# Row norms that travel as rows through DRAM instead of a second turn of the attention output

## The reference

```python
def xattn(q, k, v, Wq, Wk, Wv, Wo, bo, g):            # q = layernorm(x), k = v = ctx
    qh, kh, vh = (einsum('bcn,oc->bon', t, W) in 8 heads of 64)
    qh = softmax(qh, axis=-2) * SCALE
    kh = softmax(kh, axis=-1)
    context = jnp.einsum('bhdn,bhen->bhde', kh, vh)
    out = jnp.einsum('bhde,bhdn->bhen', context, qh)
    out = jnp.einsum('bcn,oc->bon', out, Wo) + bo[None, :, None]
    norm = jnp.maximum(jnp.sqrt(jnp.sum(out * out, axis=1, keepdims=True)), 1e-12)
    return out / norm * g * np.sqrt(DIM)

def ffn(x, c1_w, c2_w, w1, w2t):                      # x: 2048 rows of 512
    inter = xf @ c1_w.T @ c2_w.T                      # 1792 columns
    idx = argmax of each block of 32 columns
    h = relu(w1[idx] . xf)                            # 56 values per row
    return h @ w2t[idx]

x = x + xattn(layernorm(x), ctx, ctx, ...)
x = x + ffn(layernorm(x), ...)
```

## Time and profile before

| | before |
|---|---|
| median of 3 runs | 752.01 us (751.99 to 753.22) |
| profiled execution | 753.24 us, span 751.3 us |
| TensorE busy | 98% |
| VectorE busy | 83% |
| GpSimd busy | 65% |
| ScalarE busy | 53% |
| mean granted TensorE clock | 0.995 |

### The profile page before, as it was taken

How to read it: one execution, slowest core, us unless ns; L and a number is a source line. 1 busy time by engine, 2 the same in 40 slices (tenths; PEclk the granted TensorE clock), 3 DMA queues, 4 the chain that set the end, 5 groups by cost and what they waited for, 6 DMA issues and landing times.

```text
span 751.3 us, 14646 instructions
## 1 busy us (share of the span) xinstructions
PE 737.9 (98%) x5210; PEld 563.4 (75%) x5210; DVE 623.5 (83%) x910; ACT 401.7 (53%) x773; POOL 485.9 (65%) x549
## 2 busy tenths in 40 slices
PE   8999999999999999999998999999999999999998
PEld 6566565565665665666667999999898999989896
DVE  6999999999999999999968677887777878777652
ACT  4899999999999999998840111111111210211110
POOL 3789999999998888687666254543545355263420
PEclk9999999999999999999998999999999999999999
DMA  7223434334333323222211203031130312111011
GB/s 167 72 79 106 121 97 119 108 101 127 98 96 102 97 78 104 75 72 57 65 40 29 73 20 106 21 101 25 26 104 20 106 21 72 56 24 50 20 52 34
DMA packets 66376, 55.23 MB, mean 74 GB/s; under 512 B 40704, under 2 KB 49536, under 8 KB 66304
## 3 DMA queue, kind: packets, MB, share of 16 engines
q1 hardware_dynamic: 65568, 53.44, 26.0%
q10 hardware_dynamic: 736, 0.85, 0.5%
HBM read 38.52 MB, written 8.39 MB: 62 GB/s over the span
## 4 chain that ended last, share of the span: by engine, by line
PE 68%; POOL 23%; DVE 2%; SPq 2%; issue 2%; ACT 1%; DMA 1%; POOLq 0%; DVEq 0%
PE slot L1109 20%; PE po L1127 11%; PE turn L1127 11%; POOL Q L535 9%; PE po L1237 6%; PE turn L1222 4%; POOL weights_lo L484 4%; PE turn L1205 4%; PE slot L1263 3%; PE slot L1277 3%; POOL c_low L517 3%; POOL x_low L474 3%; POOL weights_hi L482 2%; SPq L276 2%; PE slot L1091 2%
## 5 line engine op out<-in xcount | busy, mean ns | idle before, releaser
L423 POOL TENSOR_TENSOR E<-E,rank 128x512 bf16<-128x512 bf16 (+1 forms) x64 | 71.0, 1110 | 110.8 <-DVE E L621 109.8
L535 POOL TENSOR_TENSOR Q<-Q,qrec 128x1024 f32<-128x1024 f32 x64 | 121.1, 1903 | 31.6 <-DVE qrec L773 31.6
L1237 PE MATMUL po<-E,ctxT 128*64 128x512 f32 x256 | 116.9, 599 | 0.0
L1240 PE MATMUL po<-QT,G 128*64 128x512 f32 x256 | 116.9, 599 | 0.0
L939 ACT ACTIVATE E<-slot,neg_kmax 128x512 f32<-128x512 f32 x128 | 86.3, 686 | 10.8 <-DVE neg_kmax L759 10.7
L725 DVE TENSOR_REDUCE qmax<-slot 128x16 f32<-128x1024 f32 x64 | 75.3, 1217 | 12.3 <-PE slot L1277 12.3
L1237 PEld LDWEIGHTS po<-E,ctxT 128*64 128x64 f32 x256 | 32.3, 136 | 64.9 <-issue 58.7
L436 POOL TENSOR_TENSOR behind<-E,first 128x512 bf16<-128x512 bf16 (+1 forms) x64 | 60.1, 941 | 31.8 <-DVE first L629 31.7
L765 DVE TENSOR_REDUCE qsum<-Q 128x16 f32<-128x1024 f32 x64 | 77.3, 1208 | 3.1 <-ACT Q L928 1.9
L759 DVE TENSOR_REDUCE neg_kmax<-slot 128x2 f32<-128x1024 f32 x64 | 76.3, 1192 | 1.0
L947 ACT ACTIVATE E<-turn 128x512 f32<-128x512 f32 x128 | 74.9, 612 | 3.1 <-PE turn L1205 2.1
(11 more groups left out here) (185 smaller groups left out, 1961.2 us busy)
## 6 DMA issues: line engine op xcount, KB each, us to landing
c_in<-in_ctx SPq DMA_DIRECT2D x64, 128.0 KB, 2.7
x_in<-in_x SPq DMA_DIRECT2D x64, 128.0 KB, 2.6
stage<-in_ffn_w SPq DMA_DIRECT2D x32, 225.0 KB, 2.6
out<-E SPq DMA_DIRECT2D x16, 256.0 KB, 2.3
ctxT<-in_ctxT SPq DMA_DIRECT2D x31, 128.0 KB, 2.4
attn_out<-po_sb SPq DMA_DIRECT2D x31, 128.0 KB, 2.3
attn<-attn_out SPq DMA_DIRECT2D x9, 256.0 KB, 3.7
E<-attn_out SPq DMA_DIRECT2D x7, 256.0 KB, 4.4
```

The costliest lines, as they stand in the source:

```text
L535: nc.gpsimd.tensor_tensor(half, half, qrec[1 - par][:, s, :].unsqueeze(2).broadcast_to([P, HALF, D]), ALU.mult).then_inc(q_scaled, 1)
L1237: nc.tensor.matmul(po[0:C, :], ctxT[1 - par][:, m, :], E[1 - par][:, :, m * P:(m + 1) * P], start=(m == 0), stop=(m == NT - 1)).then_inc(p ...
L1240: nc.tensor.matmul(po[C:P, :], G[:, m, :], QT[m][:], start=(m == 0), stop=(m == HT - 1)).then_inc(out_mm, 1)
```

## The change

The attention output is no longer scaled in its turned form and no longer turned back. It is still turned once to get the sums of squares, but ScalarE squares it in place in PSUM and VectorE reads the sums from there, ordered by batch. GpSimd's power then works on one tile (tiles 0, 1) or on two tiles at once (128x16). TensorE turns the 8 or 16 columns of factors with a single transpose (`turn_factors`), ScalarE copies them to SBUF as rows of 128 (`keep_rows`), a DMA stores them to a new DRAM tensor `factors`, and after it has landed, DMAs load them back, each row of 512 repeated over the 64 channels of its batch. VectorE (GpSimd for tiles 0 and 1) multiplies the unturned attention output by that. In the duos the two DMA trips are issued from ScalarE's queue (`exchange`), in the attention steps from SyncE's.

Orders change too. Tiles 0 and 1 begin in steps 24 and 27 (before 27 and 29), their factors travel in steps 25 and 28, and their normalization is GpSimd's. In the duos `turn_attn` of tiles a + 2 and a + 3 comes one duo earlier, after `down(d, 3)`, with squares and norms behind it; `turn_factors` stands before `hide(d, 1)`. GpSimd's `select(2)`, `rank_mask(3)` and `rank_mask(4)` move to the end of the duo before, and VectorE's order follows. SyncE's load of the next attention tiles waits for the residual, before the masks 6 and 7.

```diff
+TURNS = (B - 8, B - 5)
+        over_channels = lambda a, b: factors[a, b:b + 1].broadcast_to([C, N])
+        inverted = lambda a: a + 1 if a < 2 else 2 + a // 2
```

On SyncE:

```diff
+                def store_factor(a):
+                    sp.wait_ge(rows_kept, a + 1)
+                    sp.dma_start(rows_of(factors[a]), inv_rows[0:2 * NT, :]).then_inc(first_stored, 16)
+                def load_factor(a):
+                    sp.wait_ge(first_stored, 16 * (a + 1))
+                    for b in range(2):
+                        sp.dma_start(spread_of(a)[b * C:(b + 1) * C, :], over_channels(a, b)).then_inc(spread_in[a], 16)
...
-                    if known == B - 2:
-                        sp.wait_ge(norm_sum, 2)
+                    if known == TURNS[1] + 2:
+                        sp.wait_ge(scaled, 2)
                         load_xr(1)
...
                         sp.dma_start(scratch[g - 2], po_sb[par][C:P, :]).then_inc(stored[par], 16)
+                    if known == TURNS[0] + 1:
+                        sp.wait_ge(c2_done, C2_ITEMS)
+                        store_factor(0)
+                        load_factor(0)
+                    if known == TURNS[0] + 2:
+                        sp.wait_ge(rank_done, 1)
+                        load_attn(1)
+                    if known == TURNS[1] + 1:
+                        sp.wait_ge(added, 1)
+                        store_factor(1)
+                        load_factor(1)
...
                         for a in (2 * d + 4, 2 * d + 5):
-                            sp.wait_ge(attn_turned, a - 1)
+                            sp.wait_ge(added, a - 1)
                             load_attn(a)
```

On GpSimd:

```diff
+                def invert(a, w):
+                    pool.wait_ge(norm_max, a + w)
+                    if a > 1:
+                        pool.wait_ge(inv_turned, a // 2 + 1)
+                    nc.gpsimd.tensor_tensor(inv[:, a % 2:a % 2 + w], norm[:, a % 2:a % 2 + w],
+                                            neg_half[:].unsqueeze(2).broadcast_to([P, w, 2 * NT]),
                                             ALU.pow).then_inc(norm_inv, 1)
+                def scale(a):
+                    pool.wait_ge(spread_in[a], 32)
+                    nc.gpsimd.tensor_tensor(attn_of(a), attn_of(a), spread_of(a), ALU.mult).then_inc(scaled, 1)
...
                 def duo(d, last):
-                    rank_mask(d, 3)
-                    select(d, 2)
-                    rank_mask(d, 4)
                     select(d, 3)
                     if not last:
-                        invert(2 * d + 2)
+                        invert(2 * d + 2, 2)
                     rank_mask(d, 5)
                     select(d, 4)
-                    if not last:
-                        invert(2 * d + 3)
...
-                    if known in (B - 5, B - 3):
-                        invert((known - (B - 5)) // 2)
-                        scale_kept((known - (B - 5)) // 2)
+                    if known in TURNS:
+                        invert(TURNS.index(known), 1)
+                    if known in (TURNS[0] + 1, TURNS[1] + 1):
+                        scale(TURNS.index(known - 1))
                     if known in (B - 4, B - 2):
                         prepare((known - (B - 4)) // 2)
+                        normalize((known - (B - 4)) // 2)
```

On VectorE:

```diff
                 def duo(d, last):
-                    if d:
-                        first_max(d, 3)
+                    first_max(d, 3)
                     h_low(d, 0)
-                    if not last:
-                        norms(a)
                     first_max(d, 4)
                     block_max(d, 5)
...
                     gate(d, 2)
+                    if not last:
+                        for t in range(2):
+                            scale(a + t)
+                            residual(a + t)
+                            moments_of(a + t)
+                        normalize(a)
                     first_max(d, 6)
...
+                    gate(d, 6)
+                    if not last:
+                        block_max(d + 1, 4)
+                    if d + 2 < DUOS:
+                        norms(a + 2, pre[0])
                     h_low(d, 5)
+                    if d + 2 < DUOS:
+                        norms(a + 3, pre[1])
                     h_low(d, 6)
                     if not last:
                         gate(d + 1, 0)
...
+                    if known == TURNS[0] + 2:
+                        residual(0)
+                    if known == TURNS[1] + 2:
+                        residual(1)
...
                 steps(step)
...
                     block_max(0, 4)
+                norms(2, pre[0])
+                norms(3, pre[1])
                 gate(0, 0)
```

On ScalarE:

```diff
+                def exchange(d):
+                    a = 2 * d + 2
+                    keep_rows(a, 4 * NT, pre[0])
+                    act.wait_ge(rows_kept, d + 3)
+                    nc.scalar.dma_start(factors[a:a + 2].rearrange("a b (t n) -> (a b t) n", n=P), inv_rows[:])\
+                        .then_inc(factors_stored, 16)
+                    act.wait_ge(factors_stored, 16 * (d + 1))
+                    act.wait_ge(scaled, a)
+                    for t in range(2):
+                        for b in range(2):
+                            nc.scalar.dma_start(spread_of(a + t)[b * C:(b + 1) * C, :], over_channels(a + t, b))\
+                                .then_inc(spread_in[t], 16)
...
                     h_high(d, 0)
                     if not last:
-                        square(a, pre[0])
-                        square(a + 1, pre[1])
+                        exchange(d)
                     h_high(d, 1)
...
                     h_high(d, 5)
+                    if d + 2 < DUOS:
+                        square(a + 2, pre[0])
+                        square(a + 3, pre[1])
                     h_high(d, 6)
...
                 steps(step)
+                square(2, pre[0])
+                square(3, pre[1])
                 duos(duo)
```

On TensorE:

```diff
+                def turn_factors(a, w, bank):
+                    pe.wait_ge(norm_inv, inverted(a))
+                    if a < 2:
+                        pe.wait_ge(q_copied, HT * (TURNS[a] - 1) + 3)
+                    nc.tensor.transpose(bank[0:w * 2 * NT, 0:P], inv[:, a % 2:a % 2 + w].rearrange("p a f -> p (a f)"),
+                                        ident[:]).then_inc(inv_turned, 1)
...
                 def duo(d, last_duo):
                     a = 2 * d + 2
-                    if not last_duo:
-                        turn_attn(a, pre[0])
-                        turn_attn(a + 1, pre[1])
                     if d:
                         down(d - 1, 5)
+                    if not last_duo:
+                        turn_factors(a, 2, pre[0])
                     hide(d, 1)
...
                     hide(d, 2)
-                    if not last_duo:
-                        turn_back(a, pre[0])
-                        turn_back(a + 1, pre[1])
                     down(d, 0)
...
                     down(d, 3)
+                    if d + 2 < DUOS:
+                        turn_attn(a + 2, pre[0])
+                        turn_attn(a + 3, pre[1])
...
                     if known == B + 1:
+                        turn_attn(2, pre[0])
+                        turn_attn(3, pre[1])
                         project(0, 5)
```

More of the change, by code:

```diff
@@ L78, in real, with program @@
     return known is None or 0 <= known + shift < B
-def program(nc, A, scratch, out):
+def program(nc, A, scratch, factors, out):
     with ExitStack() as ctx:
@@ L669, in duo @@
                     gate(d, 1)
-                    if not last:
-                        scale(a + 1)
                     block_max(d, 6)
                     h_low(d, 1)
+                    gate(d, 2)
                     if not last:
-                        residual(a, pre[0])
-                    gate(d, 2)
+                        for t in range(2):
[3 more added lines that the diff above has]
+                        normalize(a)
                     first_max(d, 6)
                     if not last:
-                        residual(a + 1, pre[1])
-                    h_low(d, 2)
+                        normalize(a + 1)
                     block_max(d, 7)
-                    if not last:
-                        normalize(a)
-                        normalize(a + 1)
-                    first_max(d, 7)
                     if not last:
@@ L693, in duo @@
                         z_low(d + 1)
-                    h_low(d, 4)
+                    h_low(d, 3)
                     if not last:
```

168 lines of the change are left out of this document (74 added, 94 removed).

## The result

| | before | after |
|---|---|---|
| median of the runs, us | 752.0 (4 runs, 750.94 to 753.22) | 773.97 (4 runs, 771.82 to 776.15) |
| ratio to before | | 1.0285 (interval 1.0266 to 1.0303) |
| profiled execution, us | 753.24, span 751.3 | 776.15, span 774.3 |
| forecast | | 763.7, range 753 to 770 |

The kernel became slower, as forecast, but by 22 us instead of 11.7; the time lies above the range.

The account below looks back on a forecast made before the run. TensorE, busy 737.9 of 751.3 us, was taken to bound the kernel. Profiled 753.24 + 4.85 + 1.0 (attention, clock) + 3.0 (first duo) + 2.8 (steady duos) = 764.9, less 1.2 for the median: 763.7, range 753 to 770.

Parts of the forecast that it names:

- the price of the power of 16 columns: GpSimd in the duos: 2.9 us by a straight line through 1 and 8 columns, bounds 1.65 and 3.3.
- the landing of the factors in step 25: Attention steps: second load of half a tile issued 9.6 us into the step, landed at 12.2, when GpSimd starts scaling.
- GpSimd's normalization: Attention step 28: normalize(0) on GpSimd adds about 1.25 us, bound 1.5, ahead of the context's split.
- the attention steps 24 to 30: Waits for the factors' round trip, less turns removed: +4.85 us, plus 1.0 for the clock; bounds -1.2 and +8.
- The steady duo: Each later duo: TensorE waits 1.2 us for GpSimd's power, so +0.47 us per duo, +2.8 for six.
- the dearest power with a late clamp: Upper case for the six steady duos, power at its highest price and a clamp delayed by GpSimd: +4.7 us.
- The cheap-power rival: 16 columns cost little more than 8: steady duos -4.4 us, first duo +1.7, total 755.2; chance 15 in 100.
- Step 26: Attention step: GpSimd's late scaling of Q makes TensorE wait 1.35 us, so the step takes about 12.6 us.
- Step 29: Attention step: late load_xr(1) delays VectorE's residual and max over the queries; 15.45 us instead of 11.25, +4.2.
- The first duo: TensorE idles 7.7 us for GpSimd's power, clock 0.5 after it; turn_x at 417.6, +3.0 us with the removed pair.
- "more waits" rival: turn_x late by 1 us in each duo, GpSimd shutting out two-input passes: +6 to +7, 770; chance 10 in 100.
- the three things that would have made the direction wrong: Steps 24 to 30 under 83 us, the power of 16 columns under 2 us, or a duo period below 44.6.

Follow-up runs that it names:

- experiment 2: Kernel after with an addition in place of the 16-column power in the duos, so the factors are not inverse norms: 759.76 us, ratio 1.0098.
- experiment 5: Kernel after with TensorE's turn_factors behind hide(d, 1) instead of before it in every duo: 758.44 us, ratio 1.0081.
- experiment 4: Kernel after with the normalization of tiles 0 and 1 on VectorE instead of GpSimd: 770.58 us, ratio 1.0249.
- Experiment 3: Kernel after with spread factors of tiles 0 and 1 loaded early from rows of x, without waiting for the store (wrong numbers): 764.67 us, ratio 1.0173.
- experiment 7: Kernel after with the 16-column power split into two of 8 columns, both ahead of select(3): 765.32 us, ratio 1.0166.
- experiment 9: Kernel after with tiles 0 and 1 scaled later, turn_factors behind a hide, and first-duo maxima before norms and power in halves: 747.94 us, ratio 0.9947.
- experiment 6: Kernel after with tiles 0 and 1 scaled a step later, behind GpSimd's scaling of Q, and residuals moved later: 763.34 us, ratio 1.0148.
- experiment 1: Kernel after with GpSimd's power ahead of select(3) instead of behind it in each duo: 768.72 us, ratio 1.0229.

## Why the prediction was wrong

The direction and the places of the waits were right; terms of the sum were too small. The steps that failed are the price of the power of 16 columns (2.9 us, measured 3.35, with the clamp before it), the landing of the factors in step 25 (12.2 us into the step, measured 13.7), GpSimd's normalization (1.25 us, measured 2.10), and the chain through VectorE in step 26, which was put at nothing. In the profiles some 11.3 us are missing from the forecast: 4.3 in the attention steps 24 to 30 (+5.85 forecast, +10.2 measured), 4.0 in the six periods (+2.8 and +6.8), 2.75 in the start, which isn't the change's, and 0.3 in the rest.

**The steady duo: right mechanism, two terms too small.** Forecast were a wait of 1.2 us and a period of 45.1, measured 1.75 and 45.78. The chain up to the power was right (forecast 6.9 to 7.4 us after `project`, measured 501.31 - 493.83 = 7.48). The power was not: I took 2.9 us by the straight line through 1 and 8 columns, and 3.3 only as the bound; it is 3.35. One of the two clamps was late as well (0.63 us, the other 0.17), which I had counted half. With the wait, a period changes by -0.88 + 1.75 + x = +1.12, so the small transpose costs 0.25 and not 0.15. Six times the error of 0.65 is 3.9 us. The bound that I gave for the dearest power with a late clamp, +4.7, was added up wrong: 6.9 + 3.3 + 0.5 - 8.9 is a wait of 1.8 us, and 6 x (-0.73 + 1.8) is +6.4, close to what was measured. The cheap-power rival falls with the 3.35 us, but its arithmetic (-0.73 a duo) is what experiments 2 and 5 show.

**Step 26: a landing put too early, and a chain left out.** Forecast 12.6 us, measured 15.74. The second load of factors was issued 9.79 us into step 25, close to the 9.6 forecast, but landed 3.9 us later and not 2.6. The scaling started at 310.18 - 296.40 = 13.78 and not at 12.2, and took 1.28 and not 1.04. So TensorE waits 2.81 us for Q, forecast 1.35: that is 1.46 of the 3.14 missing. I had also followed the lateness only through GpSimd's scaling of Q. In step 29 I had followed it through SyncE, whose loads wait for `x_low`, to VectorE; in step 26 the same load feeds VectorE's statistics, which stand in front of the max over the queries, and I didn't look, since only `load_xr(1)` seemed to come behind it. What this chain adds is seen where the clock stays at 1.00 in this step, as in experiment 5 (the max over the queries, and the next keys):

```profile
315.19 2.34 DVE L753 TENSOR_REDUCE qmax<-slot 128x16 f32<-128x1024 f32 x2
```
```profile
318.81 0.50 PE L1302 MATMUL slot<-c_high,wk_hi 64*128 64x512 f32 x2 [0.44 <-DVE Q L762]
```

The keys wait for VectorE and start 3.62 us after the first maximum, in experiment 4 too. In the kernel after the maximum starts at 11.08, so without a lower clock the step would take 14.70, 0.6 more than 11.25 + 2.81. The last 1.04 us are the clock's. Experiment 3 takes away only the lateness of the factors, and step 26 is back at 11.25.

**Step 29: right chain, terms too small.** Forecast 15.45, measured 17.69. The scaling took 1.28 instead of 1.04 and began 12.85 us into step 28 instead of 12.2; the normalization took 2.10 instead of 1.25 (my bound was 1.5). So `load_xr(1)` was issued 10.0 us into the step instead of 8.35 and the max started at 13.88 instead of 12.05. From there to the keys it is 3.6 us at a clock of 1.00 (3.62 in step 29 of experiment 7), and I had 3.4. The last 0.2 is the clock's, at 0.58 over 360 to 364. I had put 1.0 in the sum for the clock; both steps together make it 1.2. That TensorE would also wait 1.74 us for `x_low` in this step was not in the forecast; it lies beside the longer chain.

**The first duo** was forecast at +3.0 and is 3.63 - 0.57 = +3.1. A wait of 7.7 us was forecast, 8.1 measured, with the clock at 0.50 behind it.

**The attention steps as a whole** were forecast at +5.85 with bounds of -1.2 and +8, and are +10.2: the outer bound assumed every landing one microsecond late, and no instruction longer than its nearest row. The range of the whole ended at 770 because I closed it at the "more waits" rival. That rival, `turn_x` late by a microsecond, doesn't happen in the kernel after: no wait at `turn_x` (L1108) is among the waits shown, and in experiment 5 there is 2.8 us of room.

**The page of the Trainium skill.** The Trainium skill, "SBUF — State Buffer", section "SBUF: two separate sides", was cited against the place in the duos: a VectorE operation with two SBUF inputs and a GpSimd operation that reads SBUF block each other for a whole instruction. It was no term of the sum. It acts, most of all in the attention steps: `residual(0)`, which now has two SBUF inputs, took 2.23 us in the kernel after. The fifteen other passes of L612 took 0.75, beside no GpSimd pass or one of a single column. The long one began at 316.80 while GpSimd scaled Q (314.73 to 318.49) and ended 0.54 after it. In the kernel before, the same pass took one input from PSUM and was not held up by the same scaling of Q (the first row is GpSimd's):

```profile
332.36 1.90 POOL L535 TENSOR_TENSOR Q<-Q,qrec 128x1024 f32<-128x1024 f32 x1 [0.59 <-DVE qrec L773]
```
```profile
333.40 0.75 DVE L586 SCALAR_TENSOR_TENSOR x<-turn,gain,x 128x512 f32<-128x512 f32 x1
```

In experiment 9 the pass with two SBUF inputs stands beside it again:

```profile
332.60 1.91 POOL L566 TENSOR_TENSOR Q<-Q,qrec 128x1024 f32<-128x1024 f32 x1 [0.58 <-DVE qrec L806]
```
```profile
333.29 1.76 DVE L616 SCALAR_TENSOR_TENSOR x<-attn,gain,x 128x512 f32<-128x512 f32 x1
```

It ends at 335.05, again 0.54 behind the end of GpSimd's pass. So the trace agrees with the Trainium skill that such a pass waits for GpSimd's to end, though it then ends 0.54 us later and not the 0.75 that it takes alone. In the duos it acts too, but is small: in six of the seven duos the first `scale`, which now has two SBUF inputs, took 0.94 to 0.97 us beside a `rank_mask` and ended 0.54 to 0.55 behind it, and in the first duo, with no GpSimd pass beside it, 0.68:

```profile
422.89 0.68 DVE L605 TENSOR_TENSOR stage<-stage,x_in 128x512 f32<-128x512 f32 x1
```
```profile
468.72 0.97 DVE L605 TENSOR_TENSOR stage<-stage,x_in 128x512 f32<-128x512 f32 x1
```

These 0.3 us vanish in the room before `turn_x`. The late clamp reads one SBUF tensor, so it is not the case that I cited, and what delays it stays open.

**Of the signs I had named**, the wait at the first small transpose, its clock, and VectorE waiting for a DMA of x in step 29 came. The steady wait and both steps were longer than said. None of the three things that would have made the direction wrong happened.

Experiment 9 removes what was added. Its span is 28.6 us below that of the kernel after (745.7 and 774.3): 10.1 in steps 24 to 30, 10.8 in the six periods, 4.8 in the first duo, and 3.3 in the start, which isn't the change's; 0.5 are lost behind step 31. The medians of experiments 5 and 6 lie 15.5 and 10.6 us below the kernel after, and experiment 9 only 26.0, though its first duo is 2.2 shorter than in experiment 5: the late start, as far as the median of the kernel after shares it, is counted in each. Against the kernel before, experiment 9 is 4.0 us shorter in the medians and 5.6 in its profile, where the six periods, each 0.68 shorter, give 4.1 and the first duo 1.2. That is nearly the 0.73 that the forecast had for the transposes taken out.

## What to carry to other kernels

Price an element-wise function on GpSimd by columns before it is put on a path: doubling its columns doubled its time, and a straight line through a tiny and a medium instruction was too kind. When an engine waits for a round trip, follow what is queued behind it through every queue that its next results release, in each place where it happens; here the chain through the loads behind `x_low` ended last in both long steps where the clock stayed up, though in step 26 it added only 0.6 us to the direct wait. A step that must be late should be moved behind independent work on the waiting engine (one hiding group, or the next scaling of Q), not ahead of other work on the producing one: moving the consumer won 1.9 us in each period and 10.1 in the attention steps; moving the producer won 0.6 in each period and sent the rest of the wait to `turn_x`. And compare more than one execution before a difference is put down to the change: 2.55 us of this profile were lost to a low clock at the start.

## What was not expected of the hardware

- GpSimd's power takes 3.35 us for 128x16 and 1.68 for 128x8, so between these two its time goes with the columns: halving it gives no gain in sum (2.02 and 1.64 in the steady duos of experiment 7), only an earlier first half.
- GpSimd's normalization of 128x512 with two scalars per partition takes 2.10 us, where VectorE needs 0.54 with no GpSimd pass beside it (experiment 4) and 1.29 beside a `select` (in each duo of the kernel after), while a product of two 128x512 tensors takes GpSimd 1.27.
- A VectorE pass of 0.75 us with two SBUF inputs took 1.76 to 2.31 where a GpSimd pass on 1024 columns was in progress, and ended 0.54 to 0.55 us behind it each time.
- Of TensorE's clock: behind the wait of 8.1 us it was 0.50 until about 418, and the six waits of 1.75 us in the duos left it at 1.00. Between these, the same wait had different outcomes. Behind the wait in step 26 it fell to 0.50 in the kernel after (2.81 us) and in experiments 1, 2 and 7 (2.73, 3.11, 2.49), and stayed at 1.00 in experiment 5 (2.71). In step 29 idle pieces of 1.74 and 2.95 us, with 2.7 us of work between them, were followed by 0.50 over 361 to 364, and in experiment 7 pieces of 1.25 and 2.95 us by 1.00.
